# Similarity products made during the edge scatter, and both partial adjacencies read by row blocks and multiplied in

## The chip, the cores and the metric

The kernel runs on one core of one Trainium2 chip. The metric is the device time of one execution in microseconds (us). Five engines run their own instruction streams and meet at semaphores: TensorE (PE in the profile; its weight loads are PEld), VectorE (DVE), ScalarE (ACT), GpSimd (POOL) and SyncE (SP, which here only issues transfers). "GB/s" and "DMA" are about the core's 16 DMA engines.

## What is computed

The input is 1250 rows of 512 numbers, 21250 directed edges (`src`, `dst`) and a weight for each edge. Two residual blocks follow one another. The first is ten steps of a propagation over the graph; the second is an LSTM over the 1250 rows in sequence, which at each row chooses one of four weight sets. Only the first block is touched by the change. Cut to what matters:

```
x0  = layernorm(x)
xn  = x0 / |x0|                                   # rows of unit length
sim = exp( <xn[src], xn[dst]> / (2 sigma^2) )     # the product is 0 where src == dst
sup = edge_weight * sim                           # one value per edge
denom = b + a * segment_sum(sup, src) + a
repeat 10 times:
    out = (x0*b + (segment_sum(sup * out[dst], src) + out)*a) / denom
x = x + out
x = x + lstm_with_selected_weights(layernorm(x))  # 1250 sequential steps
```

## The kernel before, in words

The graph part works on dense matrices. The rows are padded to 1280, which is RT = 10 blocks of 128. The weights of the edges are added into a dense 1280 x 1280 adjacency in DRAM; the kernel keeps two of them (`adj[0]`, `adj[1]`), each filled from half of the edges, and adds them later. A value that has no edge is zero, so multiplying the sum by the dense matrix of similarities gives `sup`.

**The scatter loop** takes EIT = 42 iterations with NQ = 4 columns of 128 edges each, 168 columns in all. In an iteration VectorE spreads the four columns of keys over a diagonal (`kdiag`, L684); TensorE turns each into a row of keys on all partitions (L922); VectorE compares them and finds equal keys inside the column (`same`, L687, and `junk`, L688); TensorE sums the weights of equal keys (`total`'s product, L925); VectorE makes the target addresses (`where_`, L698) and copies the sums (`total`, L700); GpSimd then issues an indirect transfer that adds them into DRAM (L364). `landed` (L372) waits for a transfer issued two before, and gives `places_free` back to VectorE, which waits for it ahead of `where_`.

**After the scatter** SyncE waits for all transfers and reads the two adjacencies whole, into `Adj` (L292) and `Adj1` (L293), 6400 KB each. VectorE waits for both (L702), adds them in ten row blocks (L704), and then, block by block, masks the diagonal of the similarity product in PSUM (L710) and multiplies the exponentials into `Adj` (L713). TensorE makes the similarity products after its part of the scatter loop (L936): for each row block three column groups (COLS: 512, 512 and 256 wide), each of four matmuls over the features, in two sets of PSUM banks, so that two row blocks can be ahead. ScalarE takes the exponential (L514) into `sim`, which holds two row blocks.

**Then** TensorE sums the columns of `Adj` for the degrees (L943), which needs all ten row blocks; VectorE forms the reciprocal of the denominator and scales `Adj` (L717 to L730), and the propagation starts (L958). The projections of the LSTM (L978) and its 1250 steps (L988 to L1011, and L1064) come last. All of that is the same before and after the change. Each engine executes in program order; there is no planner.

Of the kernel before, what the change touches and what calls it, by code (L numbers as in the profile page):

```python
# [5 lines left out]
def gnn_then_selected_lstm(  # L6
# [36 lines left out]
    NQ = 4  # L43
# [26 lines left out]
    with ctx:  # L70
# [104 lines left out]
        unit_ps = ps[:, 3, 0:TB]  # L175

# [29 lines left out]
        adj_in = sem("adj_in")  # L206
        adj_sum = sem("adj_sum")
        sim_mm = sem("sim_mm")
        sim_masked = sem("sim_masked")
        sim_exp = sem("sim_exp")  # L210
# [69 lines left out]
        def _(sp):  # L280
# [9 lines left out]
            for b in range(2):  # L290
                sp.wait_ge(scattered[b], 16 * EIT * (NQ // 2))
            sp.dma_start(Adj[:, :, :], adj[0][0:NN].rearrange("(t p n) -> p t n", p=P, n=NP)).then_inc(adj_in, 16)  # L292
            sp.dma_start(Adj1[:, 0:RT * NP].rearrange("p (t n) -> p t n", t=RT),  # L293
                         adj[1][0:NN].rearrange("(t p n) -> p t n", p=P, n=NP)).then_inc(adj_in, 16)
# [173 lines left out]
        def _(act):  # L468
# [135 lines left out]
        def _(dve):  # L604
# [74 lines left out]
            with dve.Fori(0, EIT) as i:  # L679
# [5 lines left out]
                for b in range(NQ):  # L685
                    dve.wait_ge(kr_ready[b], n)
                    dve.tensor_scalar(same[:, b, :], ps[:, 2 * b, 0:P], kcol[b], None, ALU.is_equal).then_inc(same_ready[b], 1)  # L687
                    dve.scalar_tensor_tensor(out=junk[:, b, :], in0=ps[:, 2 * b, 0:P], scalar=kcol[b], in1=below[:, :],  # L688
# [5 lines left out]
                for b in range(NQ):  # L694
                    dve.wait_ge(shift_ready[b], n)
# [3 lines left out]
                    dve.wait_ge(total_mm[b], n)  # L699
                    dve.tensor_copy(total[:, b, :], ps[:, 2 * b + 1, 0:1]).then_inc(edge_out[b], 1)  # L700

            dve.wait_ge(adj_in, 32)  # L702
            for r in range(RT):
                dve.tensor_tensor(Adj[:, r, :], Adj[:, r, :], Adj1[:, r * NP:(r + 1) * NP], ALU.add).then_inc(adj_sum, 1)  # L704
            for r in range(RT):
                c = r // 4
                q = r * P - COLS[c][0]
                dve.wait_ge(sim_mm, NCH * r + c + 1)
                blk = ps[:, 2 + 3 * (r % 2) + c, q:q + P]
                dve.tensor_tensor(blk, blk, not_ident[:, :], ALU.mult).then_inc(sim_masked, 1)  # L710
# [182 lines left out]
        def _(pe):  # L893
# [24 lines left out]
            with pe.Fori(0, EIT) as i:  # L918
                n = pe.snap(i + 1)
                for b in range(NQ):  # L920
                    pe.wait_ge(kd_ready[b], n)
                    nc.tensor.matmul(ps[:, 2 * b, 0:P], ones[:, :], kdiag[:, b, :], start=True, stop=True).then_inc(kr_ready[b], 1)  # L922
                for b in range(NQ):
                    pe.wait_ge(same_ready[b], n)
                    nc.tensor.matmul(ps[:, 2 * b + 1, 0:1], same[:, b, :], ew[:, bass.ds(i * NQ + b, 1)],  # L925
                                     start=True, stop=True).then_inc(total_mm[b], 1)

            for q in range(NQ):
                pe.wait_ge(edge_out[q], EIT)
            for r in range(RT):  # L930
                for c, (c0, m) in enumerate(COLS):
                    if r >= 2:

                        pe.wait_ge(sim_exp, NCH * (r - 2) + c + 1)
                    for k in range(KC):
# [197 lines left out]
```

## Time and profile before

| | |
|---|---|
| time, median of 3 runs | 6920.52 us (6920.15 to 6922.67) |
| profiled execution, its own time | 6914.68 us |
| its span in the trace | 6912.9 us |
| mean granted TensorE clock | 0.946 of full speed |
| scatter loop, first to last indirect transfer issued | 61.34 to 401.35 us |
| end of the scatter to the first degree product | 409.06 to 534.06 us |

Busy time says which engine works, not which one decides. A stage is read by asking what the engine that ends it last was waiting for. Times inside the trace are counted from the start of the span.

### The profile page before, as it was taken

What the parts mean: (1) busy time and instruction counts of PE and PEld (TensorE: products, weight loads), DVE (VectorE), ACT (ScalarE), POOL (GpSimd) and SP (SyncE); (2) the same over time, 40 slices, a digit from 0 to 9 for tenths busy, and PEclk for the clock granted to TensorE, in tenths of its full rate; (3) what the DMA queues carried; (4) which work ended last, traced back from release to release, by engine and by line L of the source; (5) the groups of instructions that cost most, each with busy time, mean ns of one, the idle gap of its engine ahead of it and who ended that gap; (6) DMA issues with size and microseconds to landing.
All of it is one profiled execution on the core that took longest, in us unless ns stands there. A gap on an engine that the chain in (4) does not pass through costs nothing.

```text
span 6912.9 us, 340981 instructions
## 1 busy us (share of the span) xinstructions
PE 6115.4 (88%) x126674; PEld 4120.1 (60%) x126675; DVE 3611.6 (52%) x19142; ACT 1804.0 (26%) x6561; POOL 1677.7 (24%) x4128
## 2 busy tenths in 40 slices
PE   3455999779999999999999999999999999999986
PEld 3432444466666666666666666666666666666664
DVE  5534111225555555555665565556556665565555
ACT  0001000323233232222333232333233333233321
POOL 4722111322222222222222222222222222222210
PEclk6577999759999999999999999999999999999999
DMA  3220000342122122222222222222222222222210
GB/s 93 0 76 0 0 0 0 109 120 61 56 62 62 56 61 60 61 59 61 63 64 62 60 63 60 62 62 65 59 61 63 64 64 61 60 62 62 61 52 27
DMA packets 715292, 389.82 MB, mean 56 GB/s; under 512 B 47547, under 2 KB 703291, under 8 KB 715008
## 3 DMA queue, kind: packets, MB, share of 16 engines
q1 hardware_dynamic: 684034, 369.66, 18.4%
q0 software_dynamic: 24192, 0.10, 1.0%
q10 hardware_dynamic: 7038, 19.69, 0.9%
q8 instruction: 19, 0.31, 0.0%
q14 instruction: 9, 0.07, 0.0%
HBM read 370.96 MB, written 18.38 MB: 56 GB/s over the span
## 4 chain that ended last, share of the span: by engine, by line
PE 69%; issue 6%; DVE 6%; DMA 0%; DVEq 0%; POOL 0%; ACT 0%; POOLq 0%; SPq 0%
PE ps L1002 33%; PE ps L1064 15%; PE ps L1011 8%; PE ps L995 5%; PE ps L991 4%; DVE hsum L832 2%; PE ps L988 2%; PE ps L978 2%; DVE osum L840 1%; DVE acts L850 1%; DVE gates L837 1%; DVE osum L843 1%; DVE cprod L846 0%; PE ps L967 0%; DMA out_rows<-wring 0%
## 5 line engine op out<-in xcount | busy, mean ns | idle before, releaser
L1002 PE MATMUL ps<-WH,hparts 128*2 128x384 f16 x49760 | 2292.2, 326 | 180.9 <-issue 162.7
L1002 PEld LDWEIGHTS ps<-WH,hparts 128*2 128x2 f16 x49760 | 1039.7, 83 | 1038.8 <-issue 284.4
L832 DVE TRANSPOSE_TENSOR_REDUCE hsum<-ps 128x12 f32<-128x384 f32 x1250 | 728.3, 583 | 1771.8 <-PE ps L1002 1760.6
L1064 PE MATMUL ps<-xcur,wcur 128*128 128x64 f32 x9728 | 1341.2, 281 | 87.5 <-issue 15.7
L1064 PEld LDWEIGHTS ps<-xcur,wcur 128*128 128x128 f32 x9728 | 1177.7, 191 | 275.0 <-issue 211.8
L443 POOL COPY xT<-hfull 128x4 f32 x1250 | 237.0, 190 | 3704.7 <-DVE hfull L861 3704.7
L459 POOL COPY wcur<-wring 128x512 f32<-128x512 f32 x1216 | 741.2, 610 | 447.0 <-ACT gxb L591 445.1
L1011 PEld LDWEIGHTS ps<-WH,hparts 128*2 128x2 f16 x40000 | 595.4, 83 | 353.6 <-issue 311.3
L1011 PE MATMUL ps<-WH,hparts 128*2 128x128 f16 x40000 | 774.3, 219 | 5.4 <-issue 0.6
L576 ACT ACTIVATE gx_now<-gxb 128x16 f32 x1250 | 269.8, 216 | 1830.0 <-DVE pick L826 1706.1
L958 PE MATMUL ps<-O,Adj 128*128 128x512 f16 x3000 | 650.3, 380 | 77.2 <-DVEq L738 77.2
L591 ACT ACTIVATE gxb<-ps,ubias,gscale 128x64 f32 x1216 | 561.3, 462 | 327.1 <-PE ps L1064 246.7
L579 ACT ACTIVATE acts<-gates 128x12 f32<-128x12 f32 x1250 | 265.6, 212 | 1355.8 <-DVE gates L837 1355.8
L958 PEld LDWEIGHTS ps<-O,Adj 128*128 128x128 f16 x3000 | 294.1, 98 | 433.3 <-issue 81.1
L991 PE MATMUL ps<-wselT,acts 128*1 128x4 f32 x10000 | 428.3, 166 | 16.8 <-DVE acts L850 2.0
L995 PE MATMUL ps<-owsel,tanc 128*1 128x4 f32 x10000 | 430.1, 166 | 0.0
L840 DVE TRANSPOSE_TENSOR_REDUCE osum<-ps 128x4 f32<-128x128 f32 x1250 | 385.4, 308 | 0.3 <-PE ps L1011 0.2
L744 DVE SCALAR_TENSOR_TENSOR Adj<-ps,Adj 128x512 f32<-128x512 f32 x100 | 69.2, 692 | 582.2 <-PE ps L958 582.2
L995 PEld LDWEIGHTS ps<-owsel,tanc 128*1 128x1 f32 x10000 | 327.9, 81 | 30.8
L991 PEld LDWEIGHTS ps<-wselT,acts 128*1 128x1 f32 x10000 | 313.3, 81 | 49.1 <-DVE acts L850 43.3
L581 ACT ACTIVATE otan<-osum 128x4 f32<-128x4 f32 x1250 | 256.7, 205 | 263.4 <-DVE osum L843 263.4
L364 POOL DMA_INDIRECT adjacency<-total,where_ x168 | 259.6, 1545 | 127.4 <-issue 80.4
(146 smaller groups left out, 5009.4 us busy)
## 6 DMA issues: line engine op xcount, KB each, us to landing
wring<-in_w_ih SPq DMA_DIRECT2D x1280, 256.0 KB, 2.9
gxb<-in_w_hh ACTq DMA_DIRECT2D x32, 512.0 KB, 4.4
adjacency<-Adj SPq DMA_DIRECT2D x2, 6400.5 KB, 24.7
Adj<-adjacency SPq DMA_DIRECT2D x2, 6400.0 KB, 27.2
adjacency<-total,where_ POOLq DMA_INDIRECT x168, 3.0
x_rows<-X SPq DMA_DIRECT2D x1, 2560.0 KB, 8.8
wring<-x_rows SPq DMA_DIRECT2D x10, 256.0 KB, 3.5
X<-in_x SPq DMA_DIRECT2D x1, 2304.0 KB
```

The source lines that it names most:

```text
L459: pool.tensor_copy(wcur[:, :, :], wring[:, u, :, :]).then_inc(wcur_set, 1)
L576: act.activation(gx_now[:, :], gxb[:, bass.ds(t % (2 * TB), 1), bass.ds(r * (G * SUB) - G * SUB, G * SUB)].rearrange("p t c -> p (t c)"), ...
L579: act.activation(acts[:, 0:3 * SUB], gates[:, :], ACT.Tanh, scale=1.0 / GATE_SCALE).then_inc(acts_ready, 1)
L591: act.activation(gxb[:, bass.ds(((b + 1) % 2) * TB, TB), bass.ds(i, 1)].rearrange("p t c -> p (t c)"), unit_ps, ACT.Identity, scale=gscale ...
L832: dve.tensor_reduce(hsum[:, :], gate_ps.rearrange("p (c q) -> p c q", q=32), AX.X, ALU.add, apply_transpose=True).then_inc(turned, 1)
L840: dve.tensor_reduce(osum[:, 0, :], ogate_ps.rearrange("p (c q) -> p c q", q=32), AX.X, ALU.add, apply_transpose=True).then_inc(oturned, 1)
L958: last = nc.tensor.matmul(ps[:, r % 8, :], M_parts[:, m_part, c, r * P:(r + 1) * P], old[:, o_part, c, :], start=(c == 0 and m_part + o_pa ...
L991: nc.tensor.matmul(logit_ps, acts[:, 3 * SUB + k:3 * SUB + k + 1], wselT[:, k, :], start=False, stop=False)
L995: last = nc.tensor.matmul(logit_ps, tanc[:, k:k + 1], owsel[:, k, :], start=False, stop=(k == SUB - 1))
L1002: last = nc.tensor.matmul(gate_ps[32 * j:32 * j + 2, :], hparts[:, k, :], WH[:, s * KC + k, part, j, 0:3 * P], start=(k == 0 and part == 0 ...
L1011: last = nc.tensor.matmul(ogate_ps[32 * j:32 * j + 2, :], hparts[:, k, :], WH[:, s * KC + k, part, j, 3 * P:4 * P], start=(k == 0 and part ...
L1064: last = nc.tensor.matmul(unit_ps, wcur[:, k, :], xcur[:, k, :], start=(k == 0), stop=(k == KC - 1))
```

## The change

The similarity products move from behind the scatter loop into it. TensorE's loop of 42 iterations is written out, and each of the first 30 iterations ends with one column group of the similarity product (`similarity`, four matmuls). To free PSUM banks for them the key rows now use banks 0 to 3, the four totals share bank 4, and each of the three column groups has one bank (5, 6, 7). Because the totals share a bank, VectorE waits for all four totals ahead of the first `where_` of an iteration. ScalarE writes the exponentials straight to `Adj`, which is free during the scatter. After the loop VectorE sets the diagonal of `Adj` to one, with a multiplication by the mask and an addition of the identity (the exponential of zero). SyncE reads the two adjacencies in ten row blocks each, 640 KB a transfer: the first into `Adj1`, the second into one of the two halves of `sim`, waiting for VectorE's sum of two blocks earlier. VectorE adds the two and multiplies the sum into `Adj`, block by block.

```diff
-            sp.dma_start(Adj[:, :, :], adj[0][0:NN].rearrange("(t p n) -> p t n", p=P, n=NP)).then_inc(adj_in, 16)
-            sp.dma_start(Adj1[:, 0:RT * NP].rearrange("p (t n) -> p t n", t=RT),
-                         adj[1][0:NN].rearrange("(t p n) -> p t n", p=P, n=NP)).then_inc(adj_in, 16)
+            rows = [one[0:NN].rearrange("(t p n) -> p t n", p=P, n=NP) for one in adj]
+            for r in range(RT):
+                sp.dma_start(Adj1[:, r * NP:(r + 1) * NP], rows[0][:, r, :]).then_inc(adj_in[r], 16)
+                if r >= 2:
+                    sp.wait_ge(adj_sum, r - 1)
+                sp.dma_start(sim[:, r % 2, :], rows[1][:, r, :]).then_inc(adj_in[r], 16)
...
-                    if c0 <= r * P < c0 + m:
-                        act.wait_ge(sim_masked, r + 1)
-                    if r >= 2:
-                        act.wait_ge(adj_ready, r - 1)
-                    act.activation(sim[:, r % 2, c0:c0 + m], ps[:, 2 + 3 * (r % 2) + c, 0:m], ACT.Exp,
+                    act.activation(Adj[:, r, c0:c0 + m], ps[:, 5 + c, 0:m], ACT.Exp,
                                    scale=ab[:, 3:4]).then_inc(sim_exp, 1)
...
                 for b in range(NQ):
+                    dve.wait_ge(total_mm[b], n)
+                for b in range(NQ):
                     dve.wait_ge(shift_ready[b], n)
 
                     dve.wait_ge(places_free[b], n)
                     dve.tensor_tensor(where_[:, b, :], shift[:, b:b + 1], kcol[b], ALU.add).then_inc(places_ready[b], 1)
-                    dve.wait_ge(total_mm[b], n)
-                    dve.tensor_copy(total[:, b, :], ps[:, 2 * b + 1, 0:1]).then_inc(edge_out[b], 1)
-
-            dve.wait_ge(adj_in, 32)
-            for r in range(RT):
-                dve.tensor_tensor(Adj[:, r, :], Adj[:, r, :], Adj1[:, r * NP:(r + 1) * NP], ALU.add).then_inc(adj_sum, 1)
-            for r in range(RT):
-                c = r // 4
-                q = r * P - COLS[c][0]
-                dve.wait_ge(sim_mm, NCH * r + c + 1)
-                blk = ps[:, 2 + 3 * (r % 2) + c, q:q + P]
+                    dve.tensor_copy(total[:, b, :], total_ps[b]).then_inc(edge_out[b], 1)
+
+            dve.wait_ge(sim_exp, NCH * RT)
+            for r in range(RT):
+                blk = Adj[:, r, r * P:(r + 1) * P]
                 dve.tensor_tensor(blk, blk, not_ident[:, :], ALU.mult).then_inc(sim_masked, 1)
+            for r in range(RT):
+                blk = Adj[:, r, r * P:(r + 1) * P]
+                dve.wait_ge(sim_masked, r + 1)
+                dve.tensor_tensor(blk, blk, ident[:, :], ALU.add).then_inc(diag_set, 1)
+            for r in range(RT):
+                dve.wait_ge(adj_in[r], 32)
+                dve.tensor_tensor(Adj1[:, r * NP:(r + 1) * NP], Adj1[:, r * NP:(r + 1) * NP], sim[:, r % 2, :], ALU.add).then_inc(adj_sum, 1)
                 dve.wait_ge(adj_sum, r + 1)
-                dve.wait_ge(sim_exp, NCH * (r + 1))
-                dve.tensor_tensor(Adj[:, r, :], Adj[:, r, :], sim[:, r % 2, :], ALU.mult).then_inc(adj_ready, 1)
+                dve.wait_ge(diag_set, r + 1)
+                dve.tensor_tensor(Adj[:, r, :], Adj[:, r, :], Adj1[:, r * NP:(r + 1) * NP], ALU.mult).then_inc(adj_ready, 1)
...
-            with pe.Fori(0, EIT) as i:
-                n = pe.snap(i + 1)
+            def similarity(r, c):
+                c0, m = COLS[c]
+                if r >= 1:
+                    pe.wait_ge(sim_exp, NCH * (r - 1) + c + 1)
+                for k in range(KC):
+                    last = nc.tensor.matmul(ps[:, 5 + c, 0:m], xT[:, k, r * P:(r + 1) * P],
+                                            xT[:, k, c0:c0 + m], start=(k == 0), stop=(k == KC - 1))
+                last.then_inc(sim_mm, 1)
+
+            for i in range(EIT):
                 for b in range(NQ):
-                    pe.wait_ge(kd_ready[b], n)
...
+                    pe.wait_ge(kd_ready[b], i + 1)
+                    nc.tensor.matmul(key_ps[b], ones[:, :], kdiag[:, b, :], start=True, stop=True).then_inc(kr_ready[b], 1)
                 for b in range(NQ):
-                    pe.wait_ge(same_ready[b], n)
...
+                    pe.wait_ge(same_ready[b], i + 1)
+                    nc.tensor.matmul(total_ps[b], same[:, b, :], ew[:, i * NQ + b:i * NQ + b + 1],
                                      start=True, stop=True).then_inc(total_mm[b], 1)
+                if i < RT * NCH:
+                    similarity(i // NCH, i % NCH)
```

On TensorE the place is the scatter loop. `kdiag` rows are the key products, `ew,same` rows the totals, and `ps<-xT` rows the similarity products. Before, a loop with the similarity products behind it:

```order
L922 MATMUL ps<-kdiag,ones 128x128 x4
L925 ISA
L925 MATMUL ps<-ew,same 128x1
...
L918 REGISTER_ALU
L918 COMPARE_AND_BRANCH
L936 MATMUL ps<-xT 128x512 x8
L936 MATMUL ps<-xT 128x256 x4
```

Now the same products, written out, with one column group in each iteration:

```order
L938 MATMUL ps<-ew,same 128x1 x4
L928 MATMUL ps<-xT 128x512 x4
L935 MATMUL ps<-kdiag,ones 128x128 x4
L938 MATMUL ps<-ew,same 128x1 x4
L928 MATMUL ps<-xT 128x512 x4
L935 MATMUL ps<-kdiag,ones 128x128 x4
L938 MATMUL ps<-ew,same 128x1 x4
L928 MATMUL ps<-xT 128x256 x4
```

So four similarity matmuls now stand ahead of the next iteration's key products on TensorE.

On VectorE the place is the end of a scatter iteration and what follows the loop. In brackets are the semaphores that a row waits for. Before:

```order
L698 TENSOR_TENSOR where_<-shift,key 128x1 [waits places_free0,shift_ready0]
L700 COPY total<-ps 128x1 [waits total_mm0]
...
L704 TENSOR_TENSOR Adj<-Adj 128x1280 [waits adj_in]
L704 TENSOR_TENSOR Adj<-Adj 128x1280 x9
L710 TENSOR_TENSOR ps<-ps,not_ident 128x128 [waits sim_mm]
L713 TENSOR_TENSOR Adj<-Adj,sim 128x1280 [waits sim_exp,adj_sum]
```

Now (`Adj<-Adj,sim` is the sum of the two partial adjacencies, `Adj<-Adj` the multiplication; `Adj` and `Adj1` are shown under one name):

```order
L702 TENSOR_TENSOR where_<-shift,key 128x1 [waits total_mm3,shift_ready0,total_mm2,places_free0,total_mm1,total_mm0]
L703 COPY total<-ps 128x1
...
L708 TENSOR_TENSOR Adj<-Adj,not_ident 128x128 [waits sim_exp]
L708 TENSOR_TENSOR Adj<-Adj,not_ident 128x128 x9
L712 TENSOR_TENSOR Adj<-Adj,ident 128x128 [waits sim_masked] x10
L715 TENSOR_TENSOR Adj<-Adj,sim 128x1280 [waits adj_in0]
L718 TENSOR_TENSOR Adj<-Adj 128x1280 [waits diag_set,adj_sum]
L715 TENSOR_TENSOR Adj<-Adj,sim 128x1280 [waits adj_in1]
L718 TENSOR_TENSOR Adj<-Adj 128x1280 [waits diag_set,adj_sum]
```

The first address of an iteration now waits for the last total; behind the loop, the sum and the multiplication of a row block follow each other and wait only for that block's two transfers.

On SyncE the place is the read of the adjacencies, two transfers of ten blocks before, twenty now:

```order
L297 DMA Adj<-adjacency 128x1280 [waits scattered1,scattered0]
L300 DMA sim<-adjacency 128x1280
L297 DMA Adj<-adjacency 128x1280
L300 DMA sim<-adjacency 128x1280
L297 DMA Adj<-adjacency 128x1280
L300 DMA sim<-adjacency 128x1280 [waits adj_sum]
```

From the third block on, the second adjacency's transfer waits for a sum, and the next block's first transfer stands behind that wait.

## Rows read from the trace of the kernel before

**Rows 1.** The page: busy tenths and granted clock in 40 slices.

```profile
PE   3455999779999999999999999999999999999986
DVE  5534111225555555555665565556556665565555
POOL 4722111322222222222222222222222222222210
PEclk6577999759999999999999999999999999999999
```

**Rows 2.** Stretches: busy time of the engines, granted clock, DMA share, GB/s.

```profile
core 0: us, PE busy (x) PEld busy (x) DVE busy (x) ACT busy (x) POOL busy (x), PEclk, DMA share, GB/s
57.00:61.70 4.70, 2.75 (x17) 2.38 (x18) 3.65 (x27) 0.03 (x1) 0.36 (x1) 0.98 0.00 0
61.70:396.70 335.00, 146.28 (x656) 142.78 (x656) 170.04 (x1146) 0.00 (x0) 254.27 (x165) 0.50 0.20 0
396.70:403.00 6.30, 6.27 (x8) 2.69 (x9) 0.00 (x0) 0.00 (x0) 4.95 (x4) 0.51 0.27 3
416.90:420.10 3.20, 0.28 (x2) 0.00 (x0) 0.00 (x0) 0.00 (x0) 0.00 (x0) 0.97 1.00 414
460.80:464.50 3.70, 3.70 (x5) 1.68 (x6) 1.70 (x2) 1.80 (x4) 0.00 (x0) 0.53 0.00 0
556.00:560.00 4.00, 0.00 (x0) 0.00 (x0) 3.86 (x5) 0.00 (x0) 0.00 (x0) 0.98 0.00 0
633.00:638.50 5.50, 5.48 (x14) 1.99 (x15) 0.00 (x0) 0.00 (x0) 0.00 (x0) 0.51 0.00 0
```

**Rows 3.** Timeline of one scatter iteration: start, us, engine, line [idle before].

```profile
205.89 1.54 POOL L364 DMA_INDIRECT adjacency<-total,where_  x1 [0.43 <-issue]
208.15 1.54 POOL L364 DMA_INDIRECT adjacency<-total,where_  x1 [0.72 <-issue]
209.03 0.16 DVE L698 TENSOR_TENSOR where_<-shift,key 128x1 uint32<-128x1 f32 x1 [1.72 <-POOLq L373]
209.82 2.08 PE L922 MATMUL ps<-kdiag,ones 128*128 128x128 f32 x8 [4.58 <-DVE kdiag L684]
210.00 1.57 POOL L364 DMA_INDIRECT adjacency<-total,where_  x1 [0.30 <-issue]
211.69 1.71 PE L925 MATMUL ps<-ew,same 128*128 x8
213.17 0.15 DVE L700 COPY total<-ps 128x1 f32<-128x1 f32 x1
216.21 1.54 POOL L364 DMA_INDIRECT adjacency<-total,where_  x1 [0.73 <-issue]
```

**Rows 4.** The indirect transfers (L364) by their line: durations, first and last start, landing.

```profile
L364 POOL DMA_INDIRECT adjacency<-total,where_ x168: 1538/1538/1720, 61.3 to 401.3; - x168
DMA to landing us min/median/max: 2.8/3.0/7.9
```

**Rows 5.** Timeline of the stage behind the scatter, SyncE and VectorE.

```profile
409.06 0.37 SPq L292 DMA_DIRECT2D Adj<-adjacency  x1
444.34 14.11 DVE L704 TENSOR_TENSOR Adj<-Adj 128x1280 f32<-128x1280 f32 x10 [47.76 <-DMA Adj<-adjacency]
480.57 1.49 DVE L713 TENSOR_TENSOR Adj<-Adj,sim 128x1280 f32<-128x1280 f32 x1 [5.44 <-ACT sim L514]
489.16 1.50 DVE L713 TENSOR_TENSOR Adj<-Adj,sim 128x1280 f32<-128x1280 f32 x1 [2.01 <-ACT sim L514]
534.06 2.41 PE L943 MATMUL ps<-Adj,ones 128*128 128x512 f32 x5 [2.54 <-DVE Adj L713]
```

**Rows 6.** The diagonal's mask (L710), by its line.

```profile
L710 DVE TENSOR_TENSOR ps<-ps,not_ident x10: 289/298/300, 458.4 to 531.6; 128x128 f32<-128x128 f32 x10
```

**Rows 7.** DMA issues: tiles, queue, count, size of each, median us to landing.

```profile
wring<-in_w_ih SPq DMA_DIRECT2D x1280, 256.0 KB, 2.9
```

**Rows 8.** Groups in 1529 to 6700 us, the LSTM: busy, mean ns, idle before.

```profile
L1011 PEld LDWEIGHTS ps<-WH,hparts 128*2 128x2 f16 x38684 | 574.2, 83 | 340.8 <-issue 300.7
```

More of the change, by code:

```diff
@@ L175, in gnn_then_selected_lstm @@
         unit_ps = ps[:, 3, 0:TB]
+        key_ps = [ps[:, b, 0:P] for b in range(NQ)]
+        total_ps = [ps[:, 4, b:b + 1] for b in range(NQ)]
         x_in = sem("x_in")
@@ L205, in gnn_then_selected_lstm @@
         scattered = [sem(f"scattered{b}") for b in range(2)]
-        adj_in = sem("adj_in")
+        adj_in = [sem(f"adj_in{r}") for r in range(RT)]
         adj_sum = sem("adj_sum")
@@ L209, in gnn_then_selected_lstm @@
         sim_masked = sem("sim_masked")
+        diag_set = sem("diag_set")
         sim_exp = sem("sim_exp")
@@ L686, in _ @@
                     dve.wait_ge(kr_ready[b], n)
-                    dve.tensor_scalar(same[:, b, :], ps[:, 2 * b, 0:P], kcol[b], None, ALU.is_equal).then_inc(same_ready[b], 1)
-                    dve.scalar_tensor_tensor(out=junk[:, b, :], in0=ps[:, 2 * b, 0:P], scalar=kcol[b], in1=below[:, :],
+                    dve.tensor_scalar(same[:, b, :], key_ps[b], kcol[b], None, ALU.is_equal).then_inc(same_ready[b], 1)
+                    dve.scalar_tensor_tensor(out=junk[:, b, :], in0=key_ps[b], scalar=kcol[b], in1=below[:, :],
                                              op0=ALU.is_equal, op1=ALU.mult, accum_out=earlier[:, b:b + 1]).then_inc(earlier_ready[b], 1)
@@ L916, in _ @@
             pe.wait_ge(trans_out, NTQ)
-            with pe.Fori(0, EIT) as i:
-                n = pe.snap(i + 1)
+            def similarity(r, c):
[7 more added lines that the diff above has]
+            for i in range(EIT):
                 for b in range(NQ):
-                    pe.wait_ge(kd_ready[b], n)
-                    nc.tensor.matmul(ps[:, 2 * b, 0:P], ones[:, :], kdiag[:, b, :], start=True, stop=True).then_inc(kr_ready[b], 1)
+                    pe.wait_ge(kd_ready[b], i + 1)
+                    nc.tensor.matmul(key_ps[b], ones[:, :], kdiag[:, b, :], start=True, stop=True).then_inc(kr_ready[b], 1)
                 for b in range(NQ):
-                    pe.wait_ge(same_ready[b], n)
-                    nc.tensor.matmul(ps[:, 2 * b + 1, 0:1], same[:, b, :], ew[:, bass.ds(i * NQ + b, 1)],
+                    pe.wait_ge(same_ready[b], i + 1)
+                    nc.tensor.matmul(total_ps[b], same[:, b, :], ew[:, i * NQ + b:i * NQ + b + 1],
                                      start=True, stop=True).then_inc(total_mm[b], 1)
+                if i < RT * NCH:
+                    similarity(i // NCH, i % NCH)
             for q in range(NQ):
                 pe.wait_ge(edge_out[q], EIT)
-            for r in range(RT):
[L931 to L935, printed above, removed]
-                        last = nc.tensor.matmul(ps[:, 2 + 3 * (r % 2) + c, 0:m], xT[:, k, r * P:(r + 1) * P],
-                                                xT[:, k, c0:c0 + m], start=(k == 0), stop=(k == KC - 1))
-                    last.then_inc(sim_mm, 1)
             pe.wait_ge(adj_ready, RT)
```

2 lines of the change are left out of this document (1 added, 1 removed).

## The prediction

> **What bounds the kernel now.** I read the page's 40 slices first [rows 1]. TensorE is nine tenths busy from about a fifth of the span on; that is the propagation and the LSTM, which the change leaves alone. Ahead of it lie slices of 173 us in which no engine is near full. The change acts only there, so the question is what ends each wait in the first 534 us.
>
> The scatter loop runs from 61.3 to 401.3 us [rows 4]: 168 transfers in 340.0 us, 2.04 us each, 8.14 us for an iteration of four. The timeline of one iteration says who sets this pace [rows 3]. GpSimd works 1.54 us on a transfer, so it is not full. A transfer lands 3.0 us after its start [rows 4]: the one that started at 205.89 had landed by 208.9, VectorE's address released by it starts at 209.03, and the transfer after next starts at 210.00. So two transfers take 3.0 us of landing and 1.1 us until GpSimd issues again, 4.1 us together: the loop is bound by landing and GpSimd's issue. TensorE is not: its products go from 209.82 to 213.40 (1.71 us behind 211.69), 3.6 us of 8.14, at half clock (0.50 granted, 1.2 GHz) [rows 2, 3]. VectorE is not either: its first sum is copied by 213.3, and the transfer that takes it starts at 216.21. From a release to the next transfer's start GpSimd takes 1.0 us (209.03 to 210.00), so about 1.9 us are left over there.
>
> Behind the scatter everything waits in a row [rows 5]. The read is issued at 409.06 and VectorE starts its sums at 444.34, 35.3 us later. Ten sums take 14.1 us. TensorE had two row blocks of similarity products ready by then, and the other eight come at 8.59 us a block (489.16 minus 480.57), since products, masks and exponentials follow each other. The first degree product starts at 534.06. From 409.06 this is 125.0 us.
>
> **The change part by part.**
>
> *The read and the sums.* The bytes are the same, so the transfers still need about 35.3 us if none is late. A row block of both matrices is 1.31 MB, 3.3 us at this rate, a tenth of the read. VectorE needs 1.41 us (14.11 over ten) or, alone, 1.48 us for a sum and 1.49 us for a multiplication [rows 5], so 3.0 us a block: just under the transfers. Is a transfer late because it waits for a sum? A 256 KB transfer lands after 2.9 us [rows 7]; at 3.3 us for 1280 KB, 0.66 us of it is data, so about 2.2 us are fixed (estimate). A 640 KB transfer then takes 2.2 + 1.65 = 3.9 us from issue. Sum, issue and landing make 5.4 us for two blocks (two halves of `sim`), 2.7 us a block, less than 3.3. So the transfers keep the pace, with little to spare. Behind the last landing come one sum and one multiplication, 3.0 us, and about 0.1 us to TensorE: 35.3 + 3.1 = 38.4 us in place of 125.0. **Gain 86.6 us.** Bounds: nothing less than the read's 35.3 is possible. If no two blocks overlapped, each would take 2.2 + 3.3 + 1.5 = 7.0 us, 70 us in all, and 35 us of the gain would go.
>
> *Twenty SyncE issues in place of two.* 0.37 us each [rows 5], 7.4 us in all, spread over 35 us and inside the 3.9 us above: nothing. Were each on the path, 7 us.
>
> *Masks and diagonals.* Twenty VectorE operations of the size of the old mask, 0.30 us [rows 6], 6 us. VectorE's last copy releases TensorE's similarity products at 396.7 [rows 2], 12 us before the read at 409.06, since the last transfer starts at 401.3 and one takes 7.9 us to land [rows 4, 5]. The landing hides them; without that cover they cost 6 us. They run beside GpSimd's last three issues. In the loop VectorE works beside these issues too: the one at 210.00 overlaps the diagonal spreads, and takes 1.57 us against 1.54 [rows 3]. So 0.03 us each, 0.1 us. [...]
>
> *The exponentials.* 30 on ScalarE, which is idle in the loop [rows 2], beside landings, with one bank for each column group and a whole three iterations until it is written again: nothing. VectorE waits at the first address for the fourth total. That total ends at 213.40 and the first copy of before at 213.32, so it comes 0.2 to 0.3 us later, inside the 1.9 us. Without that cover it would be 42 x 0.3 = 13 us.
>
> *The similarity products inside the loop.* This is the open price. At full clock (2.4 GHz) a row block takes 8.59 us, so a 512 group 3.44 us and a 256 group 1.72; at half clock 6.87 and 3.44. They stand ahead of the next key products, which VectorE waits for and, behind it, GpSimd. TensorE's own loop is 3.6 + 3.44 = 7.0 us at full clock, inside 8.14: free. At half clock throughout, three iterations take 10.5 + 10.5 + 7.0 = 28.0 us against 24.4, 3.6 us more, ten times, less the 1.9 us left over: 34 us. What clock is granted? Scatter work alone holds the lower level [rows 2]: it fell at 61.7 us, after 4.7 us of it, and stayed at 0.50. Unbroken products of 512 columns brought it up after 6.3, 3.7 and 5.5 us (the stretches from 396.7, 460.8 and 633.0). A group at half clock is 6.9 us of just such work, so it should end at the upper level at the latest. It stays up for 3.2 and 4.0 us after the last product (from 416.9 and 556.0). Between two groups lie 4.7 us, partly filled by small products. So the clock will be up in many iterations and fall in some. If each 512 group began low and rose after 3.7 to 6.3 us, it would take 5.3 to 6.6 us, and three iterations 24.9 to 27.4 us: 4 to 28 us in all. Held up, 0. I take 4, because only some groups begin low and a single late iteration is absorbed by the 1.9 us.
>
> *The degree products start cold.* Before, TensorE came straight from similarity products. Now it has been idle for some 50 us. By the same three stretches, 3.7 to 6.3 us go at half speed, so 1.9 to 3.2 us are lost; I take 2.6.
>
> Sum: -86.6 + 0.1 + 4 + 2.6 = -79.9. The profiled execution took 6914.7 (span 6912.9), which gives 6834.8; the median of the runs shown is 5.8 above it, so 6840.6, **6841 us** (1.2% faster).
>
> **The rivals.**
>
> *TensorE delays the scatter.* The clock falls between most groups, and the loop grows by 10 to 34 us: 6847 to 6871. For it: scatter work alone kept the clock at 0.50 for 335 us [rows 2]. Against it: every long run of 512-column products raised it. Chance 14%.
>
> *The row reads are latency-bound.* A transfer behind the wait for a sum comes later than I work out, VectorE waits at each block, and half to all of the bound of 35 us is paid: 6858 to 6876. For it: 2.7 against 3.3 us a block is a thin margin and SyncE takes transfers in order. Against it: the first five transfers are issued at once, so the queue always holds 1.6 to 3.3 us of data. Chance 9%.
>
> *Nothing, or slower.* TensorE's program grows by some 330 matmuls ahead of the LSTM, and each of its 1250 steps takes branches between four copies of the products. Now the wait ahead of the output products is 340.8 us in 38684 / 32 = 1209 steps, 0.28 us a step [rows 8]. If the copies lay worse in TensorE's instruction memory, each step would wait longer; from 80 / 1250 = 0.064 us a step on, the gain is gone, and with a doubled wait, 0.28 us, the kernel takes 7190 us. Against it: the loop's own instructions are unchanged, and the row's wait is one of every step, taken branch or not. The Trainium skill says what would make it so (Runtime: NRT & Kernel Launch, "Instruction fetch mechanics"): a taken branch whose target is outside the blocks held must fetch it first. No run here shows it yet. Chance 4%, most of it for slower.
>
> The forecast itself, 6830 to 6847: 71%. Some 2% is for what I don't see.
>
> **How the numbers follow.** The forecast's range is the sum with 0 to 8 us for the loop, 1.9 to 3.2 for the cold start and 3 us either way for the read. To hold 8 in 10 it must reach into the first two rivals: 6830 to 6860. Within 0.2% of 6920.5 is 14 us either way, about what a measurement can tell from no change. Faster by more needs under 6907; both first rivals are: 0.95. Same 0.02, slower 0.03.
>
> **What the profile after would show.** Right: first to last indirect transfer 340 to 348 us; granted clock near 1.0 in much of the first 30 iterations; no similarity product behind the loop; the first multiplication some 10 us after the read is issued and the last 38 us after it; the first degree product near 452, at half clock; from there on the same durations, shifted. Wrong: iterations of 10.5 us with granted clock 0.50 (first rival); VectorE idle for more than 1 us ahead of each sum (second); longer waits ahead of L1016 in the LSTM (third).

## The result, and the profile after

The changed kernel takes 6861.2 us, the median of four executions (6858.08 to 6865.91), against 6921.6 us (6920.15 to 6926.73) of the kernel before: a ratio of 0.9913, with a 95% interval of 0.9901 to 0.9926. That is 0.9% faster; 6841 was forecast, with 6830 to 6860 as the range. The profiled execution took 6865.91 us, with a span of 6864.2 us against 6912.9. So the two traces are 48.7 us apart where the medians are 60.4 apart: the profiled execution of before was about 7 us below its median, that of after 5 above. What follows sums the traces.

The slices of the changed kernel, to set beside [rows 1], and its instruction queue:

```profile
PE   6727999679999999999999999999999999999986
PEclk8758999579999999999999999999999999999999
q8 instruction: 28, 0.46, 0.0%
```

TensorE's first two slices, in which similarity products now run from 60 us on, are at 6 and 7 tenths; before, they were at 3 and 4. The granted clock of these two slices is 0.8 and 0.7, not near 1.0. The instruction queue moved 28 packets; the page of before has 19.

The same stretches as in [rows 2], moved with their events: the scatter with similarity products, the scatter without them, the read, the degree products.

```profile
60.60:306.00 245.40, 197.31 (x719) 129.76 (x717) 125.43 (x833) 19.77 (x31) 184.12 (x119) 0.81 0.21 1
306.00:404.80 98.80, 39.31 (x176) 38.37 (x176) 50.99 (x336) 0.00 (x0) 75.32 (x49) 0.50 0.21 0
414.20:458.60 44.40, 0.00 (x0) 0.00 (x0) 29.84 (x20) 0.00 (x0) 0.00 (x0) 0.50 0.82 296
458.60:482.50 23.90, 23.53 (x60) 12.01 (x60) 0.29 (x1) 0.00 (x0) 0.00 (x0) 0.92 0.00 1
```

By their lines, the indirect transfers, the degree products, the propagation's products, and the last operation of each LSTM step (`hfull`):

```profile
L370 POOL DMA_INDIRECT adjacency<-total,where_ x168: 1539/1539/2482, 60.6 to 404.8; - x168
L948 PE MATMUL ps<-Adj,ones x60: 379/592/1193, 458.6 to 481.8; 128*128 128x512 f32 x40, 128*128 128x256 f32 x20
L963 PE MATMUL ps<-O,Adj x3000: 379/379/634, 559.4 to 1209.3; 128*128 128x512 f16 x188
L866 DVE TENSOR_TENSOR hfull<-osig,tanc x1250: 161/163/165, 1448.1 to 6837.4; 128x4 f32<-128x4 f32 x179
```

The same two last lines of the kernel before:

```profile
L958 PE MATMUL ps<-O,Adj x3000: 379/379/634, 633.0 to 1282.9; 128*128 128x512 f16 x188
L861 DVE TENSOR_TENSOR hfull<-osig,tanc x1250: 161/163/165, 1522.3 to 6885.6; 128x4 f32<-128x4 f32 x179
```

Subtracting starts gives the account, in us of the trace:

| stretch | before | after | difference | forecast |
|---|---|---|---|---|
| start to the first indirect transfer | 61.3 | 60.6 | -0.7 | 0 |
| first to last indirect transfer | 340.0 | 344.2 | +4.2 | +4 (+0.1 masks) |
| last transfer to the read's issue | 7.7 | 9.4 | +1.7 | 0 |
| read's issue to the first degree product | 125.0 | 44.4 | -80.6 | -86.6 |
| first degree product to first propagation product | 98.9 | 100.8 | +1.9 | +2.6 |
| from there to the first `hfull` | 889.3 | 888.7 | -0.6 | 0 |
| first to last `hfull`: the LSTM | 5363.3 | 5389.3 | **+26.0** | 0 |

The propagation started 73.6 us earlier, close to the forecast. A third of that is given back in the LSTM, 1000 us behind the last changed line. Two questions are left: why the LSTM is slower, and where 6 us of the read went.

The LSTM first. Of the 26 us, 12.8 lie in the first 12 steps and 15.4 in steps 12 to 1210 (differences between the starts of the `hfull` rows of those steps). Waits of TensorE's weight loads in the steady part (steps 12 to 1210), before:

```profile
PEld ps L1011 <- issue: 298.5, 907, 0.5
PEld ps L1002 <- issue: 269.1, 291, 1.1
PEld ps L988 <- issue: 8.5, 49, 0.2
```

and after, where L1016 is the old L1011 (output products), L1007 the old L1002 (cell products) and L993 the old L988 (first logits product); the columns are us in total, times, longest:

```profile
PEld ps L1016 <- issue: 305.0, 907, 0.5
PEld ps L1007 <- issue: 278.1, 291, 1.2
PEld ps L993 <- issue: 15.8, 92, 0.2
```

"issue" means that the profile shows nothing that was being waited for; I read it as TensorE's own sequencer being late. The three grow by 6.5, 9.0 and 7.3 us. In the first steps such waits are long; this one stands 15 us behind the first `hfull` of the changed kernel:

```profile
1463.33 0.11 PEld L1007 LDWEIGHTS ps<-WH,hparts 128*2 128x2 f16 x8 [4.86 <-issue]
```

The instruction queue tells more of these first steps. Between the first `hfull` and that of step 12 it moved, in the changed kernel and then in before:

```profile
q8 instruction: 6, 0.10, 0.6%
```

```profile
q8 instruction: 1, 0.02, 0.1%
```

One of the six falls into the 4.9 us ahead of the wait's end above. In the steady steps neither kernel shows any.

No operation in the loop differs. So the theory, which is the third rival of the prediction in a milder form: **the longer program ahead of the loop has moved the loop to a worse place in TensorE's instruction memory.** Its rival: the loop starts at another moment relative to its transfers and settles into another rhythm.

For the read, VectorE's timeline shows the gaps, and SyncE's the issues of the second adjacency:

```profile
420.83 1.49 DVE L715 TENSOR_TENSOR Adj<-Adj,sim 128x1280 f32<-128x1280 f32 x1 [17.75 <-DMA sim<-adjacency]
428.82 1.49 DVE L715 TENSOR_TENSOR Adj<-Adj,sim 128x1280 f32<-128x1280 f32 x1 [1.87 <-DMA sim<-adjacency]
452.41 1.49 DVE L715 TENSOR_TENSOR Adj<-Adj,sim 128x1280 f32<-128x1280 f32 x1 [2.20 <-DMA sim<-adjacency]
457.01 1.49 DVE L718 TENSOR_TENSOR Adj<-Adj 128x1280 f32<-128x1280 f32 x1
```

```profile
414.22 0.32 SPq L297 DMA_DIRECT2D Adj<-adjacency  x1
422.35 0.32 SPq L300 DMA_DIRECT2D sim<-adjacency  x1
430.34 0.32 SPq L300 DMA_DIRECT2D sim<-adjacency  x1
```

The first sum ends at 422.32 and the transfer waiting for it is issued at 422.35; its block is summed at 428.82, 6.5 us later. The loop through the two halves of `sim` takes 430.34 - 422.35 = 8.0 us for two blocks, 4.0 us a block, more than the 3.3 us that the prediction allows a block at the read's rate.

### The profile page after: what moved, and what is told of

It reads as the page before. It is cut to its first block, busy times and chain, and to the rows that moved or that the text cites. A ratio compares the mean times of both kernels' runs of the same rounds, so it can differ in the third digit from the quotient of the medians.

```text
span 6864.2 us, 340774 instructions
## 1 busy us (share of the span) xinstructions
PE 6126.8 (89%) x126674; PEld 4106.7 (60%) x126675; DVE 3617.9 (53%) x19152; ACT 1804.5 (26%) x6561; POOL 1685.8 (25%) x4128
## 4 chain that ended last, share of the span: by engine, by line
PE 70%; issue 6%; DVE 6%; DMA 0%; DVEq 0%; SPq 0%; POOL 0%; ACT 0%; POOLq 0%
PE ps L1007 33%; PE ps L1069 15%; PE ps L1016 8%; PE ps L1000 5%; PE ps L996 4%; DVE hsum L837 2%; PE ps L993 2%; PE ps L983 2%; DVE osum L845 1%; DVE acts L855 1%; DVE gates L842 1%; DVE osum L848 1%; DVE cprod L851 0%; PE ps L972 0%; DMA wring<-in_w_ih 0%
## 5 line engine op out<-in xcount | busy, mean ns | idle before, releaser
L1007 PE MATMUL ps<-WH,hparts 128*2 128x384 f16 x49760 | 2297.3, 326 | 194.4 <-issue 173.2
L1007 PEld LDWEIGHTS ps<-WH,hparts 128*2 128x2 f16 x49760 | 1042.4, 83 | 1046.7 <-issue 297.0
L1016 PEld LDWEIGHTS ps<-WH,hparts 128*2 128x2 f16 x40000 | 596.7, 83 | 359.0 <-issue 316.6
L1016 PE MATMUL ps<-WH,hparts 128*2 128x128 f16 x40000 | 775.4, 219 | 8.6
L996 PE MATMUL ps<-wselT,acts 128*1 128x4 f32 x10000 | 439.4, 166 | 19.6 <-DVE acts L855 4.4
L749 DVE SCALAR_TENSOR_TENSOR Adj<-ps,Adj 128x512 f32<-128x512 f32 x100 | 69.2, 692 | 582.2 <-PE ps L963 582.2
L996 PEld LDWEIGHTS ps<-wselT,acts 128*1 128x1 f32 x10000 | 319.6, 81 | 57.1 <-DVE acts L855 48.0
```

What stands on the lines that cost most here:

```text
L996: nc.tensor.matmul(logit_ps, acts[:, 3 * SUB + k:3 * SUB + k + 1], wselT[:, k, :], start=False, stop=False)
L1007: last = nc.tensor.matmul(gate_ps[32 * j:32 * j + 2, :], hparts[:, k, :], WH[:, s * KC + k, part, j, 0:3 * P], start=(k == 0 and part == 0 ...
L1016: last = nc.tensor.matmul(ogate_ps[32 * j:32 * j + 2, :], hparts[:, k, :], WH[:, s * KC + k, part, j, 3 * P:4 * P], start=(k == 0 and part ...
```

## The experiments

Twelve kernels, in three groups of four, each group timed beside the kernel before. The medians of before were 6921.8, 6920.4 and 6917.4 us. LSTM columns are read from `hfull` as above, each from one trace; "steady" is steps 12 to 1210. Spans of single traces differ for another reason too: from the first propagation product to the first `hfull` it is 881 to 883 us in five of the fourteen traces and 886 to 890 in nine, with no change of code there. So compare kernels by the medians and by the columns, not by one span.

| kernel | median us | ratio [95%] | first to last transfer | LSTM | first 12 | steady |
|---|---|---|---|---|---|---|
| before | 6921.6 | - | 340.0 | 5363.3 | 56.4 | 5123.9 |
| after | 6861.2 | 0.9913 [0.9901, 0.9926] | 344.2 | 5389.3 | 69.2 | 5139.3 |
| unroll_only | 6944.0 | 1.0033 [1.0020, 1.0045] | 342.2 | 5382.8 | 65.2 | 5138.2 |
| pad246 | 6933.3 | 1.0017 [1.0008, 1.0027] | 342.8 | 5439.2 | 59.0 | 5198.7 |
| sim_behind | 6927.6 | 1.0010 [1.0000, 1.0020] | 342.8 | 5384.2 | 66.8 | 5138.1 |
| deep | 6854.1 | 0.9910 [0.9894, 0.9927] | 343.4 | 5387.7 | 66.7 | 5139.6 |
| jump755 | 6913.1 | 0.9991 [0.9981, 1.0000] | 343.8 | 5445.1 | 60.4 | 5203.6 |
| jump450 | 6837.6 | 0.9885 [0.9868, 0.9901] | 343.9 | 5366.7 | 56.8 | 5128.5 |
| best | 6838.1 | 0.9881 [0.9865, 0.9898] | 344.5 | 5388.0 | 67.0 | 5140.4 |
| best755 | 6887.2 | 0.9950 [0.9933, 0.9967] | 346.1 | 5442.3 | 59.3 | 5203.2 |
| jump194 | 6839.5 | 0.9886 [0.9869, 0.9902] | 344.3 | 5366.8 | 57.1 | 5127.5 |
| best194 | **6812.3** | 0.9850 [0.9834, 0.9867] | 345.6 | 5365.1 | 57.4 | 5127.6 |
| best130 | 6817.2 | 0.9856 [0.9839, 0.9872] | 344.6 | 5368.0 | 55.9 | 5131.2 |
| best66 | 6825.5 | 0.9869 [0.9852, 0.9885] | 345.1 | 5379.9 | 63.0 | 5137.4 |

**unroll_only: the kernel before, with only TensorE's scatter loop written out.** Nothing that the loop waits for changes, and the LSTM starts when it did.

```diff
-            with pe.Fori(0, EIT) as i:
-                n = pe.snap(i + 1)
+            for i in range(EIT):
+                n = i + 1
...
```

> The kernel before, with one edit: TensorE's scatter loop of 42 iterations is written out, so that its LSTM code lies about 1290 instructions further on, as in the changed kernel; similarity and reads as before. Theory (place of the LSTM's code): from the first to the last hfull the LSTM grows from 5363 us to about 5389, as in the changed kernel; total about 6947 us, ratio 1.004. Rival (the growth of 26 us comes from what the change moved in time, not from the code): LSTM within 5 us of 5363, total 6921, ratio 1.000. Both: 340 us from first to last indirect transfer.

The first and last `hfull` of this kernel:

```profile
L861 DVE TENSOR_TENSOR hfull<-osig,tanc x1250: 161/163/165, 1520.9 to 6903.7; 128x4 f32<-128x4 f32 x179
```

5382.8 us, 19.5 more than before, though the LSTM starts within 1.4 us of before's. The kernel is 0.33% slower; its profiled execution, 6932.0 us, was the fastest of six, so the trace shows 17 us of the 22 between the medians. The similarity products and the reads have nothing to do with this part of the loss; the written-out code alone brings most of it: 8.8 of the 12.8 us in the first 12 steps and 14.3 of the 15.4 in the steady ones. Its first-to-last transfer is also 2.2 us longer.

**sim_behind: the changed kernel, with the products behind the scatter loop again.**

```diff
-                if i < RT * NCH:
-                    similarity(i // NCH, i % NCH)
             for q in range(NQ):
                 pe.wait_ge(edge_out[q], EIT)
+            for i in range(RT * NCH):
+                similarity(i // NCH, i % NCH)
```

> The changed kernel with the similarity products all behind the scatter loop instead of in it; the row-block reads, the exponentials into Adj and VectorE's order stay. Theory (the groups on TensorE cost the scatter its 4.2 us): first to last indirect transfer 340.0 us. Rival (VectorE's wait for all four totals costs it): 344. Both: products run from about 398 us, 86 us at full clock, then masks and ten sums and multiplications, 31 us, so the first degree product comes at about 520 us; total about 6921 - 14 + 26 = 6933 us.

The first degree product starts at 525.0 us, so the products inside the loop are worth 66 us; reading by row blocks without them gains only 9 us at this point over the kernel before [rows 5], and the LSTM takes those back. The scatter takes 342.8 us with no similarity product in it, neither the 340.0 of the theory nor the 344 of its rival.

**deep: six places for the second adjacency in place of two** (four lie in `O1`, not yet in use), so that no transfer waits long for a sum.

```diff
-                if r >= 2:
-                    sp.wait_ge(adj_sum, r - 1)
-                sp.dma_start(sim[:, r % 2, :], rows[1][:, r, :]).then_inc(adj_in[r], 16)
+                if r >= 6:
+                    sp.wait_ge(adj_sum, r - 5)
+                sp.dma_start(second[r % 6], rows[1][:, r, :]).then_inc(adj_in[r], 16)
```

> The changed kernel with six places for the second adjacency's row blocks in place of two (four more in O1, which is free then), so that the wait for a sum is five blocks back. Theory (the read is bound by the wait for a sum, since a 640 KB transfer lands after 6.5 us): from the read's first issue to the first degree product 39 us in place of 44.4, total 5 us less, 6856. Rival (twenty small transfers are slower in themselves): still 44 us, total 6861.

SyncE's first issue, and VectorE's first, third and last pieces:

```profile
411.76 0.32 SPq L299 DMA_DIRECT2D Adj<-adjacency  x1
418.93 1.49 DVE L717 TENSOR_TENSOR Adj<-Adj,sim 128x1280 f32<-128x1280 f32 x1 [16.61 <-DMA sim<-adjacency]
428.36 1.49 DVE L717 TENSOR_TENSOR Adj<-Adj,O 128x1280 f32<-128x1280 f32 x1 [0.15 <-DMA O<-adjacency]
448.72 1.49 DVE L720 TENSOR_TENSOR Adj<-Adj 128x1280 f32<-128x1280 f32 x1
```

No wait for a transfer is longer than 0.15 us behind the first block, and from the issue to the first degree product (450.4) it is 38.6 us, the prediction's 38.4 within 0.2. One trace would be thin evidence, since the same stretch varies in the kernels with two places: jump450 takes 40.1 us, after and jump194 44.4 and 44.3. But the last multiplication ends 40.0 to 44.3 us after the issue in the five traces with two places and 37.8 to 39.5 us in the six with six. By the medians alone deep can't be told from after: the intervals of the two ratios overlap. The transfers' medians to landing, of the changed kernel and then of this one:

```profile
Adj<-adjacency SPq DMA_DIRECT2D x10, 640.0 KB, 7.3
sim<-adjacency SPq DMA_DIRECT2D x10, 640.0 KB, 6.5
```

```profile
Adj<-adjacency SPq DMA_DIRECT2D x10, 640.0 KB, 14.0
O<-adjacency SPq DMA_DIRECT2D x6, 640.0 KB, 15.1
```

Each transfer lands twice as late, and the whole read is 5.8 us faster: the longer landing time is queueing behind the other transfers in flight.

**pad246: 246 increments of an unused semaphore at the start of TensorE's program**, executed, so that all later code lies 246 instructions further on.

> The changed kernel with 246 more semaphore instructions at TensorE's start, where it waits for VectorE anyway, so that the LSTM's code lies at the same place within a block of 256 instructions as in the kernel before. Theory (the place within a block decides): the LSTM is back near 5363 us, total about 6836. Rival (only the amount of code ahead of it, or something else, decides): LSTM about 5389, total 6861.

I had counted that this would move the loop back to a place like that of before. It did the opposite: the LSTM took 5439.2 us, 50 more than after. The increments ran from 0.9 to 38.6 us, 0.154 us each:

```profile
L902 PEldq EVENT_SEMAPHORE  x246: 51/51/51, 0.9 to 38.6; - x123
```

Part of that lay under work that TensorE waits for anyway; the first transfer came at 78.5 us, 18 us late. As a cure it failed; as an experiment it says much, since no instruction of the loop differs. My count was off: by the instructions in the traces an iteration of before's scatter loop is 39 of TensorE's (16 products, 16 weight loads, seven for the loop and the addresses), with one more ahead of the loop; written out, the 42 iterations are 1344 and one wait. So the LSTM of before lies 1305 instructions ahead of that of after, not the 1290 of unroll_only's expectation. Its waits in the steady part (L996 is the first logits product, L1019 the output products):

```profile
PEld ps L1019 <- issue: 333.7, 907, 0.5
PEld ps L996 <- issue: 143.2, 547, 0.4
```

The wait ahead of the first logits product, 8.5 us before and 15.8 after, has become 143.2 us in 547 steps.

**jump755 and jump450: instructions that are jumped over.** A comparison that is never true stands ahead of 755 or 450 increments, between the scatter and the degree products. With the comparison's own three (a count of the program; the trace shows two of them, a move and a branch) the loop moves by 758 and 453. This takes no time worth naming, and so leaves the moment of each step alone.

```diff
+            never = pe.alloc_register("never")
+            pe.reg_mov(never, 0)
+            with pe.If_eq(never, 1):
+                for _ in range(755):
+                    pe.sem_inc(pad, 1)
...
```

> The changed kernel with 755 instructions that TensorE jumps over behind its scatter loop, so that the LSTM's code lies 2048 instructions further on than in the kernel before. Theory (what decides is the place of the loop's code within 2048 instructions, the PE instruction memory of the Trainium skill's page Runtime: NRT & Kernel Launch): the LSTM takes 5363 us again as before, its steady steps 5124 us (12th to 1210th), the total 6861 - 26 = 6835 us. Rival (any other place costs as much, or more code costs more): 5389 us or more, steady 5139 or more, total 6861 or more.

> The same with 450 instructions jumped over: by my count the loop's code then begins at a multiple of 2048 and does not cross the next one. Theory: no crossing inside the loop, so the LSTM takes about 5363 us, total 6835. Rival (it is some other address that counts, such as the place of one branch's target): neither 5363 nor 5389; a value of its own, as the 5439 us with 246 instructions more was.

The two, by the waits of the first logits product in the steady steps, jump755 first:

```profile
PEld ps L999 <- issue: 157.3, 593, 0.4
```

```profile
PEld ps L999 <- issue: 11.5, 66, 0.2
```

755 was chosen in the belief that a place repeats every 2048 instructions, and was to bring back the LSTM of before. It gave 5445.1 us: that belief fell. 450 gave the 5363 us and the 6835 that it was expected to give, within 4 us, but by luck, since its reason was the same 2048. But 758 and 246 are 512 apart, give or take one, and gave 5203.6 and 5198.7 in the steady part, which suggests that a place repeats every 256 or 512. The rival, another moment of the start, is out: the first `hfull` comes at 1448.1 us in after and at 1446.8 in jump755, and the LSTMs are 56 us apart.

**best and best755: the deep kernel, with the degree products row block by row block** (each row block is multiplied as soon as it is ready, not all ten at the end), without and with the 755.

```diff
-            pe.wait_ge(adj_ready, RT)
-            for c, (c0, m) in enumerate(COLS):
-                for r in range(RT):
+            for r in range(RT):
+                pe.wait_ge(adj_ready, r + 1)
+                for c, (c0, m) in enumerate(COLS):
```

> The changed kernel with six places for the second adjacency's blocks, and the degree products by row blocks: each block's six-matmul group starts when its multiplication is done, not when all ten are. From the read's first issue to the end of the degree products: 39 + 3 = 42 us in place of 44.4 + 23.9 = 68.3, if TensorE at half clock keeps up with a block (4.3 us of products against 3.5 us of transfers costs up to 8 us more). Total 6861 - 18 to 26 = 6835 to 6843 us.

> Both together: six places, degree products by row blocks, and the 755 instructions jumped over. If the place of the code is worth 26 us: 6809 to 6817 us. If not: as the kernel without the jump, 6835 to 6843.

The propagation of `best` starts at 533.2 us, 26 earlier than that of after, and the time is 23 us lower. With 755 the LSTM is again the slow one (5203.2 steady), and the time, 6887.2 us, fits neither branch of its expectation: the place decides in both kernels alike.

**jump194, best194, best130, best66.** 194 + 3 is 256 less than 450 + 3; if a place repeats every 256, it gives the same LSTM. The others go from it in steps of 64 towards none.

> The changed kernel with 194 instructions jumped over, 256 fewer than the 450 that gave back the 23 us. Theory (the place of the loop's code within a block of 256 instructions decides, which is also why 246 and 755 more gave the same 5199 and 5204 us: with the jump's own three they differ by 512): steady steps 5128 us, LSTM 5367, total 6838. Rival (distance, or the place within 2048): some other value, 5139 to 5204 steady.

> Six places, degree products by row blocks, 194 instructions jumped over. By the same theory 23 us less than the 6838 us without the jump: 6815 us, the fastest so far. Rival: 6838 or more.

> The same with 130 instructions jumped over, 64 before the place that is good. Theory: a value of its own, the same that any other place 64 before it would have; if the steady time changes in steps where a branch crosses a block's edge, between 5124 and 5204 us, total 6811 to 6891.

> The same with 66 instructions jumped over, 128 before the place that is good. Theory as for 130: steady 5124 to 5204 us, total 6811 to 6891; three places 64 apart and the two known ones show how wide the good stretch is.

5127.5 us steady with 194 and 5128.5 with 450: the same, and as forecast (5128, LSTM 5367, total 6838). These two shifts are exactly 256 apart, whatever the comparison itself counts. Ordered by the shift against the changed kernel, counted modulo 256, with the 16 KB packets of the instruction queue between the first `hfull` and that of step 12:

| shift mod 256 | kernels | packets | first 12 | steady |
|---|---|---|---|---|
| 0 | after, unroll_only, sim_behind, deep, best | 6 | 65.2 to 69.2 | 5138.1 to 5140.4 |
| 69 | best66 | 4 | 63.0 | 5137.4 |
| 133 | best130 | 1 | 55.9 | 5131.2 |
| 197 | jump194, jump450, best194 | 1 | 56.8 to 57.4 | 5127.5 to 5128.5 |
| 231 | before (shift of -1305, counted from the traces) | 1 | 56.4 | 5123.9 |
| 246 | pad246, jump755, best755 | 1 | 59.0 to 60.4 | 5198.7 to 5203.6 |

unroll_only and sim_behind have as many instructions of TensorE ahead of the LSTM as after, by their traces; the order and the timing of the work ahead differ, and the LSTM takes within 7 us of the same time. The first steps are long exactly where the queue moved 4 or 6 packets in them. The steady steps follow something else: of all 14 traces only those of pad246, jump755 and best755 have a packet in them, one each.

`best194` is faster than both kernels: 6812.3 us, 1.5% under before. Its degree products beside the read:

```profile
424.87 11.75 PE L956 MATMUL ps<-Adj,ones 128*128 128x512 f32 x24 [29.88 <-DVE Adj L721]
437.37 2.42 PE L956 MATMUL ps<-Adj,ones 128*128 128x512 f32 x6 [0.76 <-DVE Adj L721]
453.03 2.42 PE L956 MATMUL ps<-Adj,ones 128*128 128x512 f32 x6 [0.71 <-DVE Adj L721]
```

TensorE now waits 0.7 us for each row block of VectorE, and only the last block's products (2.4 us) stand behind the read.

## Why the prediction was wrong

The direction and the mechanism of the gain were right, and so was the likeliest case up to the start of the propagation: -73.6 us in the trace against -79.9. From forecast to trace 31.2 us are missing: LSTM 26.0, read 6.0, landing 1.7, less 2.5 from the small terms.

- **The step that failed** is the third rival's "the loop's own instructions are unchanged", taken as an argument that the LSTM stays as it is; it has no term in the sum, and 4% were given to anything else. The mechanism named there is what happened, at 26.0 / 1250 = 0.021 us a step in place of its doubled wait of 0.28. unroll_only shows it without the change's other parts, the shifts without any other code: 26 us here, up to 82 (jump755), which over 1250 steps is 0.065 us each. The text had worked out 0.064 us as the point at which the gain is gone, and jump755's ratio is 0.9991. Whether any gain was left hung on a count of instructions. "Longer waits ahead of L1016" came true in small (298.5 to 305.0 us in the steady steps); the growth ahead of the cell and the first logits products was larger (9.0 and 7.3 us). The price of the doubled wait was also read high: of the 340.8 us of [rows 8] 300.7 are named issue, 0.25 us a step.
- **The term that was mis-sized** is "a 640 KB transfer then takes 2.2 + 1.65 = 3.9 us": 6.5 us. It was worked out for a transfer alone, from a 256 KB transfer [rows 7]; here up to three others shared the engines. Two blocks took 8.0 us in place of 5.4, and the read 44.4 in place of 38.4. This is the second rival in a mild form: VectorE waited over 1 us, but at three of the nine later blocks only. deep, where the loop through `sim` is opened, gives 38.6.
- **The scatter's +4** was measured as +4.2, but largely by luck: the 4 was the price of the products. unroll_only (342.2) and sim_behind (342.8) have no similarity product in the loop and are already 2.2 and 2.8 us longer than before, so at most about 2 us are left for products and masks. The group at 81.71 below took 6.21 us, the one at 237.80 took 3.68: a row block's first 512 group took 4.8 to 6.7 us and its second 3.68, in all ten blocks, at a clock of 0.81 in the mean from 60.6 to 306 us. So half of the 512 groups ran partly at the lower level of the clock, and the loop absorbs it. The first rival did not occur.

```profile
81.71 6.21 PE L928 MATMUL ps<-xT 128*128 128x512 f32 x8
237.80 3.68 PE L928 MATMUL ps<-xT 128*128 128x512 f32 x8
```

- **The masks at 0.1 us** were wrong. GpSimd's last three issues in the changed kernel, and in jump450:

```profile
399.86 1.60 POOL L370 DMA_INDIRECT adjacency<-total,where_  x1 [0.31 <-issue]
402.01 2.48 POOL L370 DMA_INDIRECT adjacency<-total,where_  x1 [0.55 <-issue]
404.79 1.54 POOL L370 DMA_INDIRECT adjacency<-total,where_  x1 [0.30 <-issue]
```

```profile
397.91 4.13 POOL L371 DMA_INDIRECT adjacency<-total,where_  x1 [0.30 <-issue]
402.35 1.54 POOL L371 DMA_INDIRECT adjacency<-total,where_  x1 [0.30 <-issue]
404.47 1.54 POOL L371 DMA_INDIRECT adjacency<-total,where_  x1 [0.58 <-issue]
```

  and VectorE's diagonal in the changed kernel and in jump450, twenty operations without a gap:

```profile
398.95 2.11 DVE L708 TENSOR_TENSOR Adj<-Adj,not_ident 128x128 f32<-128x128 f32 x10
400.98 2.10 DVE L712 TENSOR_TENSOR Adj<-Adj,ident 128x128 f32<-128x128 f32 x10
```

```profile
396.50 2.11 DVE L709 TENSOR_TENSOR Adj<-Adj,not_ident 128x128 f32<-128x128 f32 x10
398.52 2.11 DVE L713 TENSOR_TENSOR Adj<-Adj,ident 128x128 f32<-128x128 f32 x10
```

  VectorE ends at 403.08 and 400.63; the stretched issues end at 404.49 and 402.04, both 1.41 us later, almost a whole issue (1.54). So an issue caught beside these operations did not end until they had. The one at 399.86, beside the first ten, lost 0.06 us; which of the twenty hold an issue, and in what part of it, is not settled. In unroll_only and sim_behind, which have no mask there, the last three take 1.54. The prediction took its price from an issue that overlapped the `kdiag` spreads [rows 3], which is no sample of twenty operations without a gap. One issue of the three pays, 0.9 us in the changed kernel and 2.6 in jump450, and even that does not show in the whole scatter: 344.2 and 343.9 us. The Trainium skill (SBUF — State Buffer, "Who interferes with whom") says that a VectorE instruction with two SBUF inputs, as these are, contends with a GpSimd instruction that reads SBUF. The stretched issues agree with a contention of this kind; which part of an issue it holds, no run here shows.
- **The degree products' cold start**: from the first of them to the first propagation product it is 98.9 us before and 100.8 after, at a clock of 0.92 in the products; 2.6 forecast, 1.9 measured.
- **The range** is worked out a little low. The sum with the three spreads that the text names gives 6833 to 6848, not 6830 to 6847; it makes no difference to the result.

What stays open: what makes a place bad in the steady steps (none or one transfer of instructions shows in them, and the waits named "issue" grow, in pad246 the first logits product's in about half of the steps); how the scatter's 4.2 us divide between the written-out code, the masks and the products, since pieces of 1 to 2 us come from single traces; and why the last landing took 9.4 in place of 7.7 us, which varies between 7.7 and 9.4 over these kernels. A version with the masks behind the last transfer was not tried.

## What to carry to other kernels

When a change adds or removes code ahead of a long loop with branches, give the loop's own time a row in the forecast, however far away it is: compare steps per microsecond in both traces, and try a few shifts of the program before judging the change; here they moved the median from 6837.6 to 6913.1 us, more than the change's whole gain of 60. Cost a wait for a free buffer with the landing time of transfers that share the queue, not of one alone, or make the ring deep enough that the question does not arise. "In a gap of VectorE" is not free while GpSimd writes transfers: a run of VectorE operations without a gap can hold an issue until it ends.

## What the runs showed of the hardware

- The time of 1198 steady steps of a loop with branches on TensorE goes from 5127.5 to 5203.6 us by its place alone, 1.5%. It repeats at shifts 256 apart (jump194, jump450), and at 512, to within an instruction, it differs by 5 us (pad246, jump755). The Trainium skill says that instructions come in blocks of 256 (Runtime: NRT & Kernel Launch, "Instruction fetch mechanics"); the period agrees with that block. Its stall at a branch that leaves the blocks held would show as transfers of instructions, and the whole changed run had 28 packets in that queue, none in the steady steps. So that rule fits the first steps and not the steady difference.
- The first 12 steps took 55.9 to 60.4 us where the instruction queue moved one packet in them, 63.0 with four and 65.2 to 69.2 with six, with single waits of 3 to 5 us ahead of TensorE's products.
- An increment of a semaphore on TensorE took 0.154 us (246 in a row, 0.9 to 38.6 us).
- A stretched indirect issue took up to 4.18 us in place of 1.54 beside 4.1 us of 128x128 fp32 operations on VectorE, and other issues beside them 1.60 to 1.68.
